# Bump attention and experts on one core: DVE's own tiles as two clamps, heads in staggered pairs, one DVE instruction over two tiles

## The reference

```
out_i = sum_j max(0, 1 - |z_i - z_j| / b_h) * v_j     (i: query tokens, j: key tokens, D = 16 channels a head)
x = x + layernorm(attention(layernorm(x)) / T)
x = x + layernorm(ffn(layernorm(x)))                   (64 experts, top 8, capacity 128, and one shared expert)
```

## Time and profile before

| what | value |
|---|---|
| median of 3 runs | 2274.71 us (2269.26 to 2275.46) |
| the profiled execution, first to last instruction | 2269.9 us |
| busy in it: PE, DVE, ACT, POOL | 2004.6, 1949.9, 1928.9, 972.7 us |
| first Abs tile starts, last one starts | 79.4, 1887.0 us |
| quads 0 to 3, 4, 5 to 7, 8, 9 to 11, 12, 13 to 15 | about 79 to 538, to 656, to 995, to 1106, to 1444, to 1555, to 1891 us |

### The profile page before, as it was taken

How to read it: one execution, slowest core, us unless ns; L and a number is a source line. 1 busy time by engine, 2 the same in 40 slices (tenths; PEclk the granted TensorE clock), 3 DMA queues, 4 the chain that set the end, 5 groups by cost and what they waited for, 6 DMA issues and landing times.

```text
span 2269.9 us, 30762 instructions
## 1 busy us (share of the span) xinstructions
PE 2004.6 (88%) x11838; PEld 737.5 (32%) x11838; DVE 1949.9 (86%) x2792; ACT 1928.9 (85%) x1284; POOL 972.7 (43%) x412
## 2 busy tenths in 40 slices
PE   6889989988989899987899999768999999899957
PEld 4423223222322232221222222212222224677733
DVE  4699999898999999999999999999999997644428
ACT  3599999999999999999999999999999996122214
POOL 1010010020318539533276376332774574377747
PEclk9999999999999999999999999989999999899989
DMA  6415334524421202131212030312120305698988
GB/s 224 183 42 200 122 113 130 184 92 157 158 111 33 86 22 98 38 116 56 93 33 86 22 114 24 114 65 84 33 86 24 105 3 128 166 244 233 217 221 306
DMA packets 184535, 259.27 MB, mean 114 GB/s; under 512 B 22728, under 2 KB 162632, under 8 KB 176200
## 3 DMA queue, kind: packets, MB, share of 16 engines
q1 hardware_dynamic: 169904, 237.84, 31.4%
q0 software_dynamic: 12288, 18.88, 4.5%
q10 hardware_dynamic: 2200, 0.60, 0.1%
HBM read 187.25 MB, written 70.03 MB: 113 GB/s over the span
## 4 chain that ended last, share of the span: by engine, by line
ACT 50%; PE 17%; DVE 11%; POOL 8%; DMA 7%; issue 6%; SPq 0%; POOLq 0%; DVEq 0%; ACTq 0%
ACT TB L1139 49%; PE ps L931 6%; DVE TB L1466 5%; POOL scr L1647 4%; PE ps L841 4%; DMA y_rows<-ZB 3%; PE ps L878 2%; POOL y_rows L1755 1%; DVE TB L1488 1%; DMA ZB<-zq_rows 1%; PE ps L1040 1%; DVE st L1198 1%; POOL TB L1741 1%; PE ps L986 1%; PE ps L886 1%
## 5 line engine op out<-in xcount | busy, mean ns | idle before, releaser
L1139 ACT ACTIVATE TB<-ZB,nzk 128x2048 f32<-128x2048 f32 x932 | 1776.7, 2042 | 53.6 <-DMA ZB<-zq_rows 47.7
L931 PE MATMUL ps<-TB,V 128*32 128x512 f32 x8192 | 1087.1, 624 | 182.7 <-DVE TB L1466 148.9
L1466 DVE TENSOR_SCALAR TB<-TB 128x2048 f32<-128x2048 f32 x932 | 1109.5, 1219 | 41.6 <-ACT TB L1139 40.2
L1647 POOL TENSOR_TENSOR scr<-ebase,scr 128x256 f32<-128x256 f32 x12 | 517.5, 43125 | 0.0
L931 PEld LDWEIGHTS ps<-TB,V 128*32 128x32 f32 x8192 | 188.4, 110 | 829.9 <-DVE TB L1466 498.1
L878 PE MATMUL ps<-XF,wsgu 128*128 128x512 f32 x512 | 277.0, 634 | 0.0
L1617 POOL TENSOR_SCALAR ve<-mv 128x4 f32<-128x4 f32 x44 | 50.4, 1145 | 520.1 <-DVE mv L1202 519.9
L1488 DVE SCALAR_TENSOR_TENSOR TB<-ZB,kz 128x2048 f32<-128x2048 f32 x92 | 216.6, 2354 | 0.0
L1645 POOL TENSOR_TENSOR scr<-ebase,scr 128x4 f32<-128x4 f32 x12 | 42.4, 3530 | 353.5 <-DVE scr L1332 353.5
L1171 ACT ACTIVATE ZB<-ps 128x128 f32<-128x128 f32 x64 | 17.7, 277 | 170.5 <-PE ps L1017 117.5
L878 PEld LDWEIGHTS ps<-XF,wsgu 128*128 128x128 f32 x512 | 81.9, 190 | 170.7 <-issue 169.4
(11 more groups left out here) (196 smaller groups left out, 1747.7 us busy)
## 6 DMA issues: line engine op xcount, KB each, us to landing
ZB<-zq_rows SPq DMA_DIRECT2D x64, 1024.0 KB, 7.0
scr<-fused_w SPq DMA_DIRECT2D x32, 512.0 KB, 3.5
TB<-y_rows SPq DMA_DIRECT2D x24, 512.0 KB, 8.0
TB<-in_egu_w SPq DMA_DIRECT2D x44, 256.0 KB
y_rows<-zero SPq DMA_DIRECT2D x20, 512.0 KB, 5.0
fused_w<-TB SPq DMA_DIRECT2D x4, 2048.0 KB, 14.5
scr<-fused_w SPq DMA_DIRECT2D x32, 256.0 KB, 2.7
XF<-in_x SPq DMA_DIRECT2D x24, 256.0 KB, 5.8
```

The source lines that it names most:

```text
L931: ins = pe.matmul(ps[k][32 * c:32 * c + 32, :], V[:, o:o + 32], tile(n)[:, 512 * c:512 * c + 512], start=(kb == 0), stop=(kb == KB - 1))
L1139: act.activation(tile(e), zrow(head), ACT.Abs, bias=nzk[b][:, kb * H + g:kb * H + g + 1], scale=1.0).then_inc(s_abs, 1)
L1466: dve.tensor_scalar(T, T, 1.0, 1.0, ALU.min, ALU.subtract).then_inc(s_bump, 1)
L1647: pool.tensor_tensor(E4[:, :, 0:64], view(ebase[:, 0:1], 0, [[0, 4], [0, 64]]), E4[:, :, 0:64], ALU.pow).then_inc(s_ex, 1)
```

## The change

- **Order.** The tiles of a quad no longer follow a formula. A table, `PLACES`, has one string for each quad with 35 to 37 letters: `a` is a pair of neighbouring tiles of two heads (0 and 1, or 2 and 3) of the same key block, both made by ACT; `c` is one tile that DVE makes. The pair of heads 2 and 3 lags three pairs behind that of 0 and 1. In all there are 134 c (6, 8, 6, 6 / 8, 10, 10, 8 / 8, 10, 10, 8 / 8, 10, 10, 8) and 445 a.
- **Pairs.** ACT writes the two tiles with two instructions into neighbouring places of the ring, and DVE handles both with one instruction over 4096 elements.
- **Two-clamp tiles.** A `c` becomes two entries of the ring, `c` and `m`: clamp(z, key, key + 1) and clamp(z, key - 1, key), each one DVE instruction from ZB to TB with two column operands. PE adds the first with the weights V and the second with the weights -V. Their difference is min(|d|, 1) but for a constant; the missing -1 is taken off as a sum of V over these keys, which PE computes (`S`) and DVE subtracts in `vector_quad_scale`. The ring of eight now holds 1158 entries in turn.
- **POOL** computes the key columns and the negated V blocks of a quad (`pool_keys`, semaphore `s_own`) into a new buffer `held`.
- **Ends of quads.** The four copies to cT stand four and two entries before the end of the quad and two and four after it.
- Some times in `timetable` move by one or a few places; the row loads (`zb`) stand in another order.

```diff
+LAG = 3
+PLACES = [
+    "acaaacaacaaaaaaaaaacaaaaacaacaaaaaa",
...
+    "acaaacaacaaacaacaacaacaaaaacaccaaaaaa",
...
 def rest_at(blk):
-    return 52 + 48 * blk
+    return 51 + 49 * blk
...
+    for i in range(4):
+        pe += [(64 * i + 10, ("S", 4 * b + i))]
+        dv += [(64 * i + 18, "S", 4 * b + i)]
...
-            s = 64 * ((n - NZB) % H // 4) + 61 + (n - NZB) % 4
+            s = 64 * ((n - NZB) % H // 4) + (57, 58, 62, 63)[n % 4 - 2]
...
+            if kind == "m":
+                pe.wait_ge(s_own, q + 1)
+            pe.wait_ge(s_bump, bump_by[e])
...
+            w = view(negated(q, quads[q][0].index(kb)), D * j, [[1, 32]]) if kind == "m" else V[:, o:o + 32]
             for c in range(4):
-                ins = pe.matmul(ps[k][32 * c:32 * c + 32, :], V[:, o:o + 32], tile(n)[:, 512 * c:512 * c + 512],
-                                start=(kb == 0), stop=(kb == KB - 1))
+                ins = pe.matmul(ps[k][32 * c:32 * c + 32, :], w, tile(e)[:, 512 * c:512 * c + 512],
+                                start=(first_of[q, j] == e), stop=(last_of[q, j] == e))
...
+                    if kind != "a":
+                        vector_clamp(n)
+                    elif n % 2:
+                        T = view(tile(n - 1), 0, [[1, 2 * NT]])
+                        dve.wait_ge(s_abs, abs_by[n])
                         dve.tensor_scalar(T, T, 1.0, 1.0, ALU.min, ALU.subtract).then_inc(s_bump, 1)
...
+        def vector_clamp(e):
...
+            if kind == "c":
+                dve.wait_ge(s_own, q + 1)
+                dve.wait_ge(q_zb[head % NZB], 16 * (head // NZB + 1))
...
+            low = 1 if kind == "c" else 0
+            dve.tensor_scalar(tile(e), zrow(head), key_column(q, low, i), key_column(q, low + 1, i),
+                              ALU.max, ALU.min).then_inc(s_bump, 1)
...
+            pool_keys(0)
+            pool_keys(1)
             for b in range(NB):
                 if b:
                     for k in range(4):
                         pool_minus(k, 4 * (b - 1) + k, p, 1e-5 * NT * NT)
+                    pool_keys(4 * b + 1)
                     for k in range(4):
                         pool_rstd(k, s_xmv, 4 * (b - 1) + k + 1, s_xrs, p)
                         if k:
                             pool_weights(b - 1, k - 1)
                         pool_route(b - 1, k)
+                        if k != 2:
+                            pool_keys(4 * b + (2, 3, 0, 4)[k])
...
+        def pool_keys(q):
...
+            if q >= 2:
+                pool.wait_ge(*tile_used(max(e for e in range(begin[q - 2], begin[q - 1]) if E[e][1] == "m")))
+            for which in range(3):
+                pool.tensor_scalar(view(key_column(q, which, 0), 0, [[4, m], [1, 4]]),
+                                   view(nzk[b][:, 0:1], own[0] * H + 4 * (q % 4), [[H, m], [1, 4]]),
+                                   -1.0, float(which - 1), ALU.mult, ALU.add)
...
+            pool.tensor_scalar(view(negated(q, 0), 0, [[64, m], [1, 64]]),
+                               view(V[:, 0:1], own[0] * C + 64 * (q % 4), [[C, m], [1, 64]]),
+                               -1.0, None, ALU.mult).then_inc(s_own, 1)
```

More of the change, by code:

```diff
@@ L25 @@
 WEIGHTS = {"fst": 10, "fn": 7, "xT": 7, "v": 7, "z": 8, "zT": 3, "cst": 10, "cn": 7, "xst": 10, "hn": 7, "hT": 7, "lg": 4,
[L26 to L49, removed]
+           "rm": 15, "re": 8, "sc": 14, "sm": 5, "sg": 4, "gu": 7, "dn": 4, "S": 2}
@@ new lines, in plan, with filled @@
+def plan():
+    return [filled(q, s, s.count("c")) for q, s in enumerate(PLACES)]
+def filled(q, order, clamps):
+    rows = (clamps + 3) // 4
+    kbs = list(range(KB - rows, KB)) if q % 4 == 3 else list(range(rows))
+    own = [(kb, j) for kb in kbs for j in range(4)]
+    own = own[:clamps]
+    first = [("a", kb, 0) for kb in range(KB) if (kb, 0) not in own]
+    second = [("a", kb, 2) for kb in range(KB) if (kb, 2) not in own]
+    tiles = first[:LAG]
+    a_, b_ = first[LAG:], second
+    while a_ or b_:
+        if a_ and len(a_) >= len(b_) - LAG:
+            tiles.append(a_.pop(0))
+        else:
+            tiles.append(b_.pop(0))
+    tiles, cl = iter(tiles), iter(own)
+    return kbs, own, [next(cl if o == "c" else tiles) if o == "a" else ("c",) + next(cl) for o in order]
@@ L52, in view, with entries @@
+def entries():
+    o = []
+    for q, (kbs, own, slots) in enumerate(plan()):
+        for kind, kb, j in slots:
+            if kind == "a":
+                o += [(q, "a", kb, j), (q, "a", kb, j + 1)]
+            else:
+                o += [(q, "c", kb, j), (q, "m", kb, j)]
+    return o
 def view(a, offset, dims):
@@ L309, in build @@
         bt = bw[:, 1:4, :]
-        kz = sb("kz", [128, 2, C])
+        held = sb("held", [128, 512])
+        Sq = [sb(f"Sq{i}", [128, 64]) for i in range(2)]
+        one = sb("one", [128, 1])
         ib = sb("ib", [128, H + 1])
@@ L336, in build @@
         use, _ = bank_uses()
[L337 to L339 removed]
+        quads, E = plan(), entries()
+        begin = [[e[0] for e in E].index(q) for q in range(4 * NB)] + [len(E)]
+        first_of, last_of = {}, {}
+        for e, (q, kind, kb, j) in enumerate(E):
+            first_of.setdefault((q, j), e)
+            last_of[q, j] = e
+        abs_by = list(itertools.accumulate(e[1] == "a" for e in E))
+        used_by = list(itertools.accumulate(last_of[e[0], e[3]] != i for i, e in enumerate(E)))
+        bump_by = list(itertools.accumulate(e[1] != "a" or i % 2 == 1 for i, e in enumerate(E)))
+        bump_by = [bump_by[i + 1] if e[1] == "a" and i % 2 == 0 else bump_by[i] for i, e in enumerate(E)]
+        s_abs, s_bump, s_used, s_own = sem("s_abs"), sem("s_bump"), sem("s_used"), sem("s_own")
         q_zb = [sem(f"q_zb{i}") for i in range(NZB)]
@@ L463, in routing, with place, negated, key_column @@
                     view(base, o + 804, [[1, 4]]), view(base, o + 808, [[1, 4]]), view(b64, o + 812, [[1, 512]]))
[L465 to L469, removed]
+        def place(e):
+            q = E[e][0]
+            return 64 * (q % 4) + sum(E[i][1] != "m" for i in range(begin[q], e))
+        def negated(q, i):
+            return view(H0, 208 * (q % 2) + 64 * i, [[1, 64]])
+        def key_column(q, which, i):
+            return view(H0, 416 + 36 * (q % 2) + 12 * which + i, [[1, 1]])
         def row_used(o):
-            tiles = [256 * (o // H) + 64 * (o % H // 4) + 4 * kb + o % 4 for kb in range(KB)]
-            ends = [[n for n in tiles if (n in own) == e][-1:] for e in (False, True)]
-            return [distances(n[0]) for n in ends if n]
+            mine = [e for e in range(begin[o // 4], begin[o // 4 + 1]) if E[e][3] == o % 4]
+            a = max(e for e in mine if E[e][1] == "a")
+            m = max(e for e in mine if E[e][1] == "m")
+            return [(s_abs, abs_by[a]), (s_bump, bump_by[m])]
         def piece_done(t):
@@ L809, in tensor_part @@
                 pe.wait_ge(empty[bank], m)
-            if what == "xT":
+            if what == "S":
+                kbs, own, _ = quads[b]
+                for kb in kbs:
+                    o, w = kb * C + 64 * (b % 4), 16 * sum(h == kb for h, _ in own)
+                    ins = pe.matmul(out_[:, 0:w], view(one[:, 0:1], 0, [[0, 128]]), V[:, o:o + w], start=(kb == kbs[0]),
+                                    stop=(kb == kbs[-1]))
+                ins.then_inc(full[bank], 1)
+            elif what == "xT":
                 pe.wait_ge(s_fn, 4 * b + k + 1)
@@ L942, in tensor_program @@
                     tensor_stage(unit)
+            upper = [min(e for e in range(begin[4 * b], begin[4 * b + 4]) if E[e][2] >= 8) for b in range(NB)]
             for b in range(NB):
```

181 lines of the change are left out of this document (103 added, 78 removed).

## The result

The changed kernel takes 2280.84 us in the median (2280.12 to 2290.94, 7 runs), the one before 2271.76 (2266.49 to 2275.46, 7 runs): a ratio of 1.0049, 95% interval 1.0035 to 1.0063. It is slower by half a percent where 1.7% faster was forecast. The profiled execution has a span of 2279.5 us against 2269.9.

The account below looks back on a forecast made before the run. ACT's Abs bound the middle; after the change PE would, narrowly, in ten quads. Stage bounds of 1732 us plus 16, 19 and 3 gave 1770, 40 less than 1809.6: span 2230, median 2235 us, range 2203 to 2290.

Parts of the forecast that it names:

- The prices of the instructions: Per-instruction costs: Abs 1.893 us, pair 2.21, clamp 1.26, PE tile 0.95, a couple's second tile 0.86.
- the sums of demand: Each engine's work after the change, by stage; quads 9 to 11: ACT 320, PE 325, DVE 314 us.
- the sum by stage: Middle of the kernel: the largest engine demand of each stage taken as its time, 1732 us against 1793 today.
- what the sum leaves out: Additions to the middle's 1732 us: 16 beside ACT's sum, 19 for uneven PE work, 3 for late keys; 1770 us.
- the bounds: Greatest demand per stage: quads 0 to 3 435 us, quad 4 108.5, quads 8 and 12 106 each, gate stages 325.
- Item (2): Gate quads: PE work is uneven and the ring evens little; 82.9 us a block against 81.3, twelve blocks 19 us.
- the rival that ends slower: The ring of four groups becomes the bound; middle 1838 us, 2303 in all if half the trips take 13.2; chance 0.17.
- my own sign for it: Sign for the ring as bound: ACT's idle time in the middle exceeds 80 us.
- the 12.5 of the rival: Mean ring trip in us above which today's time is passed; the forecast had 12.2.
- The late keys (3 us): Starts of quads 8 and 12: DVE waits about 3 us in all for POOL's key columns.
- The rival with PE at its upper price: PE tiles at 0.99 and 1.06 us: quads 9 to 11 need 338 us, whole 2250 to 2275; chance 0.15.
- For POOL: Rival: wide DVE instructions double POOL's delay, keys 8 us later at two starts, 2250 us; chance 0.05.

Follow-up runs that it names:

- (1): Changed kernel with pairs undone: DVE handles each of ACT's tiles by an instruction of its own (singles); 2263.9 us, ratio 0.997 to the kernel before.
- 12: Singles with 122 couples and V loads 11 to 15 later in SP's queue, quad 4 cut from 8 couples to 4 late ones; 2249.66 us, ratio 0.991.
- 13: Fastest version (singles, 118 couples, four late ones in quad 4) with the pairs put back on DVE; 2270.85 us, ratio 1.0002.
- (4): Kernel before with the pairs alone: 420 wide DVE instructions, order and own tiles as they were; 2310.92 us, ratio 1.0177.
- (7): Version with single instructions, 8 couples for 10 in six gate quads, 122 in all; 2256.03 us, ratio 0.9936.
- 5: Changed kernel with PE's matmuls for the couples' second tile left out (one of 16 columns stays); 2257.08 us, ratio 0.993.
- 6: Changed kernel with the second clamp on DVE cut to 512 of its 2048 elements; 2257.33 us, ratio 0.9926.
- 11: Changed kernel with both cuts: PE's second-tile matmuls left out and DVE's second clamp cut to 512 of 2048 elements; 2224.34 us, ratio 0.9799.
- (15): Fastest version with 4 couples in place of 8 and 6 in quads 1 and 2, outside the z stretches; 2251.75 us, ratio 0.9911.

## Why the prediction was wrong

*What held.* The prices of the instructions. The wide instruction starts the next one 2.20 us later (forecast 2.21), a clamp from ZB has 1343 ns as the form of line 1464 had 1350, the second tile of a couple starts the next after 0.88 us (forecast 0.86), 890 Abs run at 1.89 us when they run at all. For ACT and DVE the sums of demand held too: 323.8 us ACT busy in quads 9 to 11 for 320, 313.6 DVE for 314.

*Two steps failed.* The first is PE's demand in the sum by stage. I counted the trace of the changed kernel again, each PE instruction from its start to the next start, or to its own end where PE then stands. In quads 9 to 11 the tiles cost 207.6 us, 0.95 each, as forecast; the rest costs 125.7 where the sum had 117.3 + 1.5. So PE needs 333 us there for 325, 331 in quads 5 to 7, 333 in 13 to 15, and 113 for 108.5 in quad 4: 27 us short in all. The fault is in the subtraction. The busy time of line 931 alone holds the tails that overlap the gate work; taken off whole, it took some 8 us of other work with it, and the tiles were put back at the smaller start-to-start price. The same sum for the kernel before gives 117.3 + 192 x 0.95 = 300 us, where the earlier trace rows have 317.9 busy; about 9 of these 18 us are PE's time at the lower clock there, the rest is the double subtraction.

The second is the step called "what the sum leaves out": 38 us beside the bounds, for 92 measured (1823.6 - 1732). With PE's need as counted the bounds come to 1758, and 65 us lie beside them: 22 in batch 0 (8 in the kernel before, above ACT's need), 13 in quad 4, 8 in quads 8 and 12, 22 in the nine gate quads. I took the greatest of three demands for the time of a stage and added little, since ACT had stayed so close to its own sum. But there PE had 6% of slack or more in each stage and DVE 4% or more, and the ring had eight separate steps. The change took PE's slack in the gate quads (94% busy before, 98% now) and made the ring's steps coarser; DVE got more slack, not less. Item (2), for uneven PE work, does not come out of its own figures either: 82.9 us are for 49 places, and 81.3 for 48, so that hardly any of its 19 us is left. What the runs put in place of the 38 us:

- The pairs cost 17 us in the changed kernel (1), 21 in the best version (12 and 13), and 40, partly for another reason, in the one before (4). I had listed their ring trip as the rival that ends slower, at 0.17, and my own sign for it came true: ACT stood over 80 us for PE. The mechanism was in the list, yet it is only part of the loss: with singles the middle is still at 1805 us. (A mean trip of 4 x 1823.6 / 579 = 12.6 us against the 12.5 of the rival is the length of the middle said another way, and no measure of the trips.)
- Couples where PE is full cost more than the Abs that they save: 8 us for 12 couples (7), 6.5 us for 4 fewer and the rest later in quad 4 (12). For quad 4 I had averaged PE over the quad. Its 32 z pieces of 1.16 us stand in the first 48 places, and that part alone needs some 85 us of PE. A demand averaged over a stage hides this.
- PE and DVE both hold the gate quads up (5, 6, 11), with the clock as a rival for part of it. The block sum of item (2) counted PE against ACT and let DVE be free.

*Smaller points.* The late keys (3 us) did not come: POOL was through at 993.1 us, 13 us before PE's first tile of quad 8 at 1006.7, the four new operations took about 1 us in all and nothing waits for `held`. The rival with PE at its upper price is not it, though PE's need comes near its 338: tiles behind a tile came at 0.86 to 0.88, and it was the other work that was larger. For POOL the picture is mixed. The mean of the first small operation of a reciprocal root rose from 1836 to 2580 ns with wide instructions and was 1878 with singles, which agrees with the Trainium skill's rule (SBUF — State Buffer, Who interferes with whom). But the operation behind it, in the same root, went from 2578 to 2406 and 3496 ns, the other way, and the small one of line 1645 from 3530 to 4646 and stayed at 4676 with singles. In the middle DVE stood 18.6 us for POOL, 11.0 with singles and 7.2 before; what of that cost time, no run shows.

*Open.* Batch 0 gained nothing in any version whose work is complete (454.8 before, 454.9 to 460.6 with a ring of eight or nine), though in most of them ACT has 6 tiles fewer there. With work left out it took 451.0 (5) and 446.1 (11). The turns between the z stretch (PE) and the statistics (DVE) are argued from the timeline and not shown by a run; (15) only shows that the number of couples isn't it. Of the 92 us, 27 are PE's mis-sized demand, 17 belong to the pairs, and up to 15 to couples in the wrong place, which overlaps with the 27. The rest I put down to the engines' turns because of (11), without a run that prices it alone.

## What to carry to other kernels

Take an engine's demand in one measure throughout, and put the sum to the kernel that you have first: start-to-start prices added to what is left of a busy time do not mix, and here the sum misses the kernel before by 18 us in one stage, half of which no clock explains. When one engine is full and the others are not, the slack of the others and the depth of the ring between them keep it full (two of eight places were worth 12 us before the change and 81 after it). So a change that takes slack and coarsens the ring's steps should, as I read these runs, be priced by stretches as short as the ring (here some 12 us), not by stages. An instruction over two buffers saved 0.07 us here (2.20 us for 2 x 1.135) and pays with two buffers held for the whole of both; it cost 17 to 21 us in a ring of eight. And when work is moved to balance sums, look where the receiving engine is already full: four couples taken out of such a stretch, and the rest moved behind it, brought about as much as twelve elsewhere.

## What was not expected of the hardware

Taking work away from PE did not take away as much PE time. In run 5, 28 tiles of about 0.8 us less in quads 9 to 11 should have cut PE's busy time by 22 us; it fell from 333.9 to 321.4, by 12.5. The granted clock of that stretch was 0.97, where it is 1.00 in the changed kernel: in all, PE ran 17.1 us of it at the lower level of 1.2 GHz, which costs 8.5 us of work at the full level of 2.4 GHz. Run 11 confirms the size: it leaves out the same work of PE, had the clock at 1.00 in these quads, and PE was busy 312.8 us, 21.1 less. What makes the clock fall is shown less well. In quad 8, where PE has the least work, it is 0.91 in both kernels (the earlier trace rows and the windows above). That agrees with the Trainium skill (TensorE: Matmul & The Clock Gate, Part 1), by which an idle array loses its full clock. But run 11 left PE idle for 14.2 of 327 us, run 5 for 16.6 of 338, and only run 5 lost clock there, so less work does not always mean a lower clock. A fuller PE did come with a better one: 0.978 for 0.962 over the whole. The three gate stages of the kernel before have 20.5, 17.1 and 17.1 us at the lower level and those of the changed one none. Half of that, 27 us, came back to PE, against some 74 us that the couples' 84 tiles of 0.88 us put on it there.
